# The gram of a tile two tiles behind its transposes, in a gathered DLRM tower

## What is computed

```python
e = jnp.stack([tbl_0[ids[:, 0]], ..., tbl_31[ids[:, 31]]], axis=1)   # 512 x 32 x 256
dots = jnp.einsum('bnd,bmd->bnm', e, e)
z = dots[:, iu, ju]                                                  # pairs i < j
h = jnp.concatenate([z, dense_ctx], axis=1)                          # 512 x 512
h = jnp.maximum(h @ W_top1 + b_top1, 0.0)
h = jnp.maximum(h @ W_top2 + b_top2, 0.0)
y = h @ W_top3
```

## Time and profile before

| | us |
|---|---|
| median of 3 runs | 251.21 |
| lowest, highest | 251.07, 251.59 |
| profiled execution, its span on the core | 251.4 |
| PE busy | 166.6 |
| POOL busy | 121.6 |
| DVE busy | 69.8 |
| ACT busy | 57.1 |

### The profile page before, as it was taken

How to read it: one execution, slowest core, us unless ns; L and a number is a source line. 1 busy time by engine, 2 the same in 40 slices (tenths; PEclk the granted TensorE clock), 3 DMA queues, 4 the chain that set the end, 5 groups by cost and what they waited for, 6 DMA issues and landing times.

```text
span 251.4 us, 6104 instructions
## 1 busy us (share of the span) xinstructions
PE 166.6 (66%) x2544; PEld 113.4 (45%) x2544; DVE 69.8 (28%) x253; ACT 57.1 (23%) x193; POOL 121.6 (48%) x132
## 2 busy tenths in 40 slices
PE   0431076666667994766667995666665974779976
PEld 0211043333335962433335973333333952447765
DVE  0000014151515025151515015151515014244331
ACT  2000003131313113131313113131313123134231
POOL 4777365556566155656666146666565235600000
PEclk9999999999999996555555597555555596555989
DMA  5833223222322112322322112222222112200000
GB/s 138 286 105 106 76 70 94 83 80 85 87 85 83 38 51 80 92 82 83 85 81 82 42 42 83 83 83 83 81 83 89 44 42 85 86 23 3 4 0 0
DMA packets 7766, 18.91 MB, mean 75 GB/s; under 512 B 2593, under 2 KB 3489, under 8 KB 7618
## 3 DMA queue, kind: packets, MB, share of 16 engines
q0 software_dynamic: 6144, 16.79, 22.9%
q1 hardware_dynamic: 1602, 1.84, 2.4%
HBM read 18.62 MB, written 0.00 MB: 74 GB/s over the span
## 4 chain that ended last, share of the span: by engine, by line
PE 63%; DVE 18%; another core or an unknown queue 7%; issue 6%; DMA 3%; ACT 2%; POOL 0%; DVEq 0%; ACTq 0%
PE xt_ps L274 28%; PE gram_ps L287 19%; PE mlp_ps L306 9%; DVE z L183 9%; DVE xt L175 7%; PE mlp_ps L317 4%; PE mlp_ps L297 2%; DMA rows<-in_table,row_number 2%; DVE slots L193 1%; ACT xt L175 1%; ACT slots L238 1%; DMA ids_sb<-in_ids 1%; POOL rows L165 0%; PE mlp_ps L325 0%
## 5 line engine op out<-in xcount | busy, mean ns | idle before, releaser
L165 POOL DMA_INDIRECT rows<-in_table,row_number x128 | 121.4, 948 | 98.6 <-PE xt_ps L274 68.1
L287 PE MATMUL gram_ps<-xt 128*32 128x32 f32 x2048 | 57.6, 238 | 68.1 <-DVE xt L175 50.6
L287 PEld LDWEIGHTS gram_ps<-xt 128*32 128x32 f32 x2048 | 40.7, 142 | 110.2 <-DVE xt L175 59.8
L274 PE MATMUL xt_ps<-identity,rows 128*128 128x128 f32 x256 | 81.9, 418 | 12.8 <-DMA rows<-in_table,row_number 9.8
L175 DVE COPY xt<-xt_ps 128x256 f32<-128x256 f32 x64 | 27.2, 425 | 156.7 <-PE xt_ps L274 136.8
L175 ACT COPY xt<-xt_ps 128x256 f32<-128x256 f32 x64 | 23.9, 373 | 121.1 <-PE xt_ps L274 89.2
L274 PEld LDWEIGHTS xt_ps<-identity,rows 128*128 128x128 f32 x256 | 35.6, 191 | 21.4 <-issue 12.8
L183 DVE COPY z<-slots 32x32 f32<-32x32 f32 x160 | 34.2, 214 | 2.5
L183 ACT COPY z<-slots 32x32 f32<-32x32 f32 x96 | 23.4, 244 | 4.3 <-DVE slots L193 2.9
L306 PE MATMUL mlp_ps<-z,w1z_sb 128*128 128x128 f32 x128 | 23.1, 364 | 1.9 <-DVE z L183 1.9
L306 PEld LDWEIGHTS mlp_ps<-z,w1z_sb 128*128 128x128 f32 x128 | 22.4, 276 | 2.7 <-issue 2.7
(11 more groups left out here) (6 smaller groups left out, 1.8 us busy)
## 6 DMA issues: line engine op xcount, KB each, us to landing
rows<-in_table,row_number POOLq DMA_INDIRECT x128
w1z_sb<-in_w1z SPq DMA_DIRECT2D x1, 1024.0 KB, 5.0
w_sb<-in_w SPq DMA_DIRECT2D x1, 512.0 KB
ids_sb<-in_ids SPq DMA_DIRECT2D x1, 64.5 KB, 1.8
identity<-in_eye SPq DMA_DIRECT2D x1, 64.0 KB, 1.9
upper_sb<-in_takes_upper SPq DMA_DIRECT2D x1, 64.0 KB, 1.9
ctx_sb<-in_ctx_t SPq DMA_DIRECT2D x1, 32.0 KB
w1c_sb<-in_w1c SPq DMA_DIRECT2D x1, 32.0 KB
```

The costliest lines, as they stand in the source:

```text
L165: nc.gpsimd.indirect_dma_start(rows[:, n % SLOTS, :], None, table, bass.IndirectOffsetOnAxis(ap=row_number[:, n:n + 1], axis=0),).then_inc ...
L274: last = nc.tensor.transpose(xt_ps[g % 2][:, k, :], rows[:, g % SLOTS, k * P:(k + 1) * P], identity[:])
L287: last = nc.tensor.matmul(gram_ps[u % 2][F * j:F * j + F, g % UNIT, :], x, x, start=(k == 0), stop=(k == KD - 1))
```

## The change

On PE the gram of tile g - 2 follows the transposes of tile g, where it was the gram of tile g - 1. At the start of a quarter the grams of the two last tiles of the quarter before follow the transposes of places 0 and 1. After the last quarter two grams are left instead of one. The waits inside `transposes`, `gram`, `layer1` and the rest are the same, as are the programs of the other engines and all buffers.

```diff
             def quarter(t, first, last):
                 for g in range(G):
                     transposes(t, g, first)
-                    if g:
-                        gram(t, g - 1, first)
+                    if g >= 2:
+                        gram(t, g - 2, first)
                     elif not first:
-                        gram(t - 1, G - 1, False)
+                        gram(t - 1, G - 2 + g, False)
                     if not first:
                         if g == LAYER1:
                             layer1(t - 1)
...
             quarters(nc.tensor, quarter)
+            gram(NQ - 1, G - 2, False)
             gram(NQ - 1, G - 1, False)
             layer1(NQ - 1, last=True)
```

## The result

| | before | changed |
|---|---|---|
| median, us | 251.14 (4 runs) | 262.24 (4 runs) |
| lowest, highest | 250.95, 251.59 | 259.59, 263.27 |
| ratio, 95% interval | 1 | 1.0428, 1.0367 to 1.0489 |
| span of the profiled execution | 251.4 | 260.0 |

The account below looks back on a forecast made before the run. Bound: a loop in which gathers hold PE's completions, 1.56 us a tile. Terms 0 - 1.17 + 0 + 0 - 0.29 = -1.46 us took the median 251.21 to 249.8; own range 248.8 to 250.8, whole range 246.0 to 253.2.

Parts of the forecast that it names:

- What bounds the kernel: Between MLP stages: gathers hold PE's completions, a loop of 3.12 us for two tiles, 1.56 each; PE's own work 1.01.
- (a): Steady rounds: transposes start 0.40 us earlier, hidden behind gathers; 0 us, bounds 16 gained or 1.1 lost through longer trains.
- (b): Three MLP stages: layer1 and the restarting gather come 0.39 us earlier each; 1.17 us gained, bounds 0 and 2.6.
- (c): Unit boundaries: eighth gram 0.2 us later, hidden by 1.46 us slack; cost 0, bound 2.2 us, 0.62 each uncovered.
- Rival 3: Unit boundaries: eighth gram may miss its release, delaying take_lower, spread, DVE's copy and gathers; 252 to 254 us; chance 0.25.
- (d): Start, first 20 gathers: PE's order changes nothing that could be priced; 0, with up to 3 us of gain.
- (e): End, after the gathers: last gram's 0.23 us wait filled, gram 127 earlier; 0.29 us gained, bounds 0 and 0.52.
- Rival 1: Steady rounds: completions follow the issue, so earlier transposes count; 234 us in full, 245 in the likelier partial form; chance 0.15.
- The rule against the trace: Skill page says PE and ACT never wait on anyone; trace shows 2.24 us against 0.78; the rule would give Rival 1's sum.

Follow-up runs that it names:

- e14: Changed kernel with half grams (second 128 of 256 features left out), paced way: 244.35 us, 0.9706 of the kernel before, 0.993 of that kernel with half grams.
- e6: Changed kernel fetching only the first 16 tiles' rows, 112 of 128 gathers left out: 208.00 us, 0.8255 of the kernel before.
- e11: Changed kernel with each unit's eighth gram as early as before, other grams two tiles behind, paced way: 253.14 us, 1.0025 of the kernel before.
- e15: Changed kernel unaltered, run in the free way: 203.95 us, 1.0332 of the kernel before.
- e1: Changed kernel with each unit's eighth gram as early as before, other grams two tiles behind, free way: 192.25 us, 0.9711 of the kernel before.
- e7: Same kernel as e1 (eighth gram as early as before), repeated in another group, free way: 191.17 us, 0.9549 of the kernel before.
- r1_before: Kernel before, unaltered, run again with a trace in a paced group: 255.93 us (one run).
- r2_after: Changed kernel, unaltered, run again in the same paced group as r1_before: 262.73 us, 1.0366 of the kernel before.

## Why the prediction was wrong, point by point

**What bounds the kernel: right, for this way of running.** Two gathers, completions held, 1.56 us a tile (1.58 when each stretch is counted from gather start to gather start: 125.0/79). A second way, in which PE sets the pace, shows in no row of the trace before, and I had not considered that the kernel might have it.

**(a) Steady rounds: right.** Predicted 0; measured 3.02 to 3.16 us a round between the stages, where it was 3.09 to 3.28, up to some 2.9 us gained over the whole kernel. The direction of the small bound was wrong (longer trains don't cost), the argument that the gathers hide the transposes' earlier start was right.

**(b) MLP stages: the mechanism right, its sign overruled.** layer1 did start a gram sooner behind its transposes' release: 83.52 - 82.03 = 1.49 us after DVE's copy, where it was 80.45 - 78.56 = 1.89. But that copy stands behind a spread, and came 2.19 us later (the table's row for tile 31). The stage lost 2.06 us besides the clock, where 0.39 was to be gained. I had costed the stage apart from the boundary right ahead of it (tiles 31 and 36), though (c) was about that very copy.

**(c) Unit boundaries: this is the step that failed.** The sentence was that the last gram "completes behind both transposes instead of between them, I estimate 0.2 us later", from the distance of two copies in one batch. That assumed it was in the batch. It was not: PE stopped in the middle of it, and `take_lower` came 3.93 us after the gram's start, not 1.71. DVE's copy was 2.2 to 2.7 us late instead of 0.1 to 0.2. Even where no gram was cut (tiles 79 and 87) it was 1.77 late, since the gram itself started 1.3 and 1.4 us later against the gathers; the slack hid that. The slack that I had worked out, 1.46 us, was near what the table shows, about 1.9. So the place and the threshold were right and the lateness was wrong by more than ten times. How much of it is the stop and how much the order, no run separates: e14 shows a gram that missed its release whole. The uncovered price of 0.62 us was exact, in e6.

**Rival 3 was the right one**, mechanism and place, at 0.25. It was priced with (c)'s 0.2 to 0.4 us of delay instead of a missed release, which by its own "if it misses the batch's release" was the price to take: a release later is up to a round, 3.12 us, less the 1.46 of slack 1.66, and for 11 boundaries 18 us. That is above what came, since the lateness was 2.2 to 2.7 us and a quarter's boundaries escaped, but a range that held it would have held 262. The argument against it, that PE had issued all four groups of a round 1.2 us before the release, was read from a round whose last piece was two transposes. The changed round ends in 16 matmul records and as many weight loads.

**(d) Start: right.** Gather 20 went out 2.87 us earlier, close to the 3 us of the bound, and gather 22 gave it all back. **(e) End:** the wait of 0.23 us ahead of the last gram is gone, as said. The 0.29 us didn't come: from the last gather to L306 of the last quarter it takes 22.09 us, where it took 21.97, and gram 127 starts 0.96 us after transposes 127 as before (0.95). Behind that L306 took 1.03 us longer at its clock.

**Rival 1 was rejected by the right rows.** The completions did not follow the issue; e11, which keeps the new order and loses little by it, stays at 1.0025 in the paced way. In the free way they do follow it, and the change costs 3.3% there, so that rival's gain didn't come there either.

**The rule against the trace.** From the start of transposes to their copy it takes 2.24 us in the paced way and 0.73 in the free one. The Trainium skill, page "SBUF — State Buffer", section "Who interferes with whom", says that PE never waits on anyone. In the free way the trace is in line with it, with gathers going out all the time (in e15 transposes at 47.65 and their copy at 48.38, gathers at 47.12 and 48.37); in the paced way PE's completions come late, which the prediction took for a contradiction. The page's sentence is about engines that contend for SBUF, and no row shows where the completion is held, so this case doesn't show that sentence to be wrong.

## What to carry to other kernels

When an edit makes some piece the last one of a batch that is released together, ask first whether it still makes the batch, and take for the bad bound one whole release less the slack of what follows, not a fraction. Follow the one instruction whose consumer feeds back into the loop (here the eighth gram, through the spread and one xt copy), and reorder around it: keep it early and move the rest. And cost a stage together with the boundary just ahead of it.

## What the runs showed of the hardware

**Two ways of running the same program.** 196 to 200 us in three groups of runs, 250 to 256 in the others, on one chip in two groups one after the other. What differs in the traces is whether PE's completions reach the other engines while gathers are issued (2.24 us from transposes to copy, or 0.73). Nothing in the kernel selects it that I know of; what does stays open. A few tenths of a per cent mean little beside it, and a change can be worth -3% in one way and nothing in the other (e1, e7, e11).

**PE stops before its work is done being issued.** In the changed kernel's cut rounds the records from the round's start to the stop are 2 + 16 + 2 + 13 = 33 matmul records after tile 23 and 2 + 16 + 2 + 9 = 29 after tile 31, with as many weight loads, give or take one: 66 and 59 instructions, with no completion seen by another engine in between. The Trainium skill, page "TensorE: Matmul & The Clock Gate", gives an engine queue depth of 64 in its table; these two counts lie on either side of it. It isn't shown to be the cause: a round of the kernel before has 36 matmul records with no visible stop, and e11 stops after fewer, 2 + 21 = 23 after tile 23. With half grams, whose whole round has 20, no eighth gram was cut.

**The clock of layer1.** The starts of the same 32 records of L306 spanned 3.53 to 6.5 us from one execution to another, as more or fewer of them stood 213 ns apart, not 112, and the sum over four quarters differed by 4.3 us between r1_before and r2_after. In the last quarter of r2_after all but the first stand 112 apart, at a granted clock of 1.00. A comparison of two single traces of this kernel has to take that out first.
